# Own-side attention scores of the edges from three bf16 parts and a bf16 one-hot instead of fp32

## The reference

```python
h_all  = einsum('nf,rof->rno', x, W).reshape(8, n, 8, 32)    # per relation
scores = sum(h_all[type, src] * attn_src, -1) + sum(h_all[type, dst] * attn_dst, -1)
scores = where(scores > 0, scores, 0.2 * scores)
amax   = maximum(segment_max(scores, dst), 0)
w      = exp(scores - amax[dst])
out    = segment_sum(h_all[type, src] * (w / segment_sum(w, dst)[dst]), dst)
```

## Time and profile before

| what | value |
|---|---|
| median of three runs (lowest, highest) | 4628.5 us (4625.87, 4634.31) |
| the profiled execution's own time | 4635.05 us |
| its span, first to last instruction | 4633.4 us |
| mean granted TensorE clock | 0.831 |
| busy share: PE, PEld, DVE, ACT, POOL | 71%, 53%, 44%, 14%, 25% |
| relation tables, 2517 to 2725 us | PE 192.66 us busy of 208, granted clock 0.97 |
| edge attention, 2784 to 4040 us | PE 809.72, DVE 793.18, POOL 783.77 us busy of 1256, granted clock 0.70 |

### The profile page before, as it was taken

How to read it: one execution, slowest core, us unless ns; L and a number is a source line. 1 busy time by engine, 2 the same in 40 slices (tenths; PEclk the granted TensorE clock), 3 DMA queues, 4 the chain that set the end, 5 groups by cost and what they waited for, 6 DMA issues and landing times. The chain is left out here.

```text
span 4633.4 us, 52170 instructions
## 1 busy us (share of the span) xinstructions
PE 3299.1 (71%) x14322; PEld 2434.7 (53%) x14323; DVE 2036.0 (44%) x4300; ACT 655.7 (14%) x1334; POOL 1159.8 (25%) x1246
## 2 busy tenths in 40 slices
PE   0899789859939223999908981577677767737998
PEld 0666578648827222777704451455455545525555
DVE  5999700220051650000033612666666766733333
ACT  0111200020022111232201320000000000012222
POOL 2700100000010204000041407466666666200000
PEclk9999899979969656999958995677777767757999
DMA  2522244234400002112130316244444334100000
GB/s 97 225 98 95 82 142 127 85 93 130 131 10 0 0 3 104 60 56 65 50 104 36 133 79 130 82 119 119 111 116 121 115 111 118 55 32 21 14 14 28
DMA packets 311385, 383.64 MB, mean 83 GB/s; under 512 B 42672, under 2 KB 255489, under 8 KB 307841
## 3 DMA queue, kind: packets, MB, share of 16 engines
q1 hardware_dynamic: 240642, 221.16, 14.5%
q0 software_dynamic: 49040, 140.22, 10.7%
q10 hardware_dynamic: 21616, 21.21, 1.5%
HBM read 270.97 MB, written 111.53 MB: 83 GB/s over the span
## 5 line engine op out<-in xcount | busy, mean ns | idle before, releaser
L1955 POOL DMA_INDIRECT att_ring<-relation_rows,table_row x784 | 784.1, 1000 | 438.5 <-issue 223.2
L2071 PE MATMUL att_acc<-att_ring,att_onehot 128*128 128x264 f32 x1568 | 532.9, 480 | 198.1 <-issue 187.5
L2071 PEld LDWEIGHTS att_acc<-att_ring,att_onehot 128*128 128x128 f32 x1568 | 358.7, 238 | 328.9 <-issue 266.1
L446 PE MATMUL counts_acc<-onehot_lo,onehot_key 128*128 128x400 bf16 x2000 | 361.7, 336 | 43.7 <-DVE onehot_key L428 43.7
L425 DVE TENSOR_SCALAR onehot_lo<-node_ids,source_lo 128x800 bf16<-128x800 int16 x1000 | 366.0, 570 | 0.0
L446 PEld LDWEIGHTS counts_acc<-onehot_lo,onehot_key 128*128 128x128 bf16 x2000 | 267.7, 139 | 141.9 <-DVE onehot_key L428 83.4
L625 PE MATMUL agg_agg<-x_gnn,agg_slab 128*128 128x257 f32 x1250 | 278.6, 382 | 66.3 <-DMA agg_slab<-edge_counts 66.3
L625 PE MATMUL agg_agg<-xn,agg_slab 128*128 128x257 f32 x1250 | 277.8, 381 | 22.5 <-DMA agg_slab<-edge_counts 22.5
L625 PEld LDWEIGHTS agg_agg<-x_gnn,agg_slab 128*128 128x128 f32 x1250 | 238.6, 191 | 102.5 <-DMA agg_slab<-edge_counts 66.7
L2034 PE MATMUL att_po<-att_near,att_onehotT 128*128 128x64 f32 x1568 | 239.8, 308 | 66.6 <-issue 63.9
L625 PEld LDWEIGHTS agg_agg<-xn,agg_slab 128*128 128x128 f32 x1250 | 237.9, 190 | 58.5 <-DMA agg_slab<-edge_counts 22.9
(11 more groups left out here) (390 smaller groups left out, 4443.6 us busy)
## 6 DMA issues: line engine op xcount, KB each, us to landing
agg_slab<-edge_counts SPq DMA_DIRECT2D x50, 1600.0 KB, 7.4
edge_counts<-counts_out SPq DMA_DIRECT2D x100, 400.0 KB
relation_rows<-tab_out SPq DMA_DIRECT2D x25, 1056.0 KB
att_targets<-targets SPq DMA_DIRECT2D x28, 896.0 KB
wide_w<-L_ffn_W ACTq DMA_DIRECT2D x14, 1024.0 KB, 6.7
att_ring<-relation_rows,table_row POOLq DMA_INDIRECT x784
expert_rows_in<-blank_rows POOLq DMA_DIRECT2D x34, 256.0 KB
expert_rows_out<-blank_rows POOLq DMA_DIRECT2D x33, 256.0 KB
```

The lines of the kernel that those rows point to most:

```text
L446: mm = nc.tensor.matmul(acc[:, k, h, 0:HALF_LO], oh_key[:, k, :, j], oh_lo[:, k, j, h * HALF_LO:(h + 1) * HALF_LO], start=False, stop=Fals ...
L1955: nc.gpsimd.indirect_dma_start(slots(p)[:, j, :], None, rows_of, bass.IndirectOffsetOnAxis(ap=c.row[:, n:n + 1], axis=0)).then_inc(landed[ ...
L2071: mm = nc.tensor.matmul(acc[:, 0:RW], oh[:, j, :], slots(p)[:, j, :], start=j == 0, stop=False)
```

## The change

The near scores are kept as three bf16 parts whose sum is the fp32 number: the first is the score rounded to bf16, the second the rest rounded, the third what then remains. GpSimd makes them in `relation_tables` from a new buffer `rest` (three copies that cast, two subtractions, each waiting for the one before), and issues its stagings two tiles ahead of the split. The rows of `target_scores` grow from 64 fp32 to 192 bf16 numbers, and SyncE stores them after a new wait, `split`. In `attend` the one-hot `ohT` is bf16, and a chunk's product becomes three bf16 matmuls that accumulate in the same place of `po`. Nothing else of the edge attention is changed.

```diff
@@ relation_tables
-        near = g.sb(ctx, f"{name}_near", [P, 2, sc])
-        beyond = g.sb(ctx, f"{name}_beyond", [P, sc])
+        near = g.sb(ctx, f"{name}_near", [P, 2, 3, sc], BF16)
+        rest = g.sb(ctx, f"{name}_rest", [P, 2, sc])
+        beyond = g.sb(ctx, f"{name}_beyond", [P, 3 * sc], BF16)
...
             @block.gpsimd
             def _(pl):
-                def step(t, b):
+                def stage(t, b):
                     pl.wait_ge(turned, t + 1)
                     nc.gpsimd.tensor_copy(st[:, b, :], tile_of(xn, t)).then_inc(staged, 1)
-                tiles(pl, NT, step)
+
+                def parts(t, b):
+                    link = chain(pl, link_s, t * 4)
+                    pl.wait_ge(read, (t + 2) * banks)
+                    pl.wait_ge(stored[b], (t - b) * 16 + 32)
+                    link(nc.gpsimd.tensor_copy(near[:, b, 0, :], rest[:, b, :]))
+                    link(nc.gpsimd.tensor_tensor(rest[:, b, :], rest[:, b, :], near[:, b, 0, :], ALU.subtract))
+                    link(nc.gpsimd.tensor_copy(near[:, b, 1, :], rest[:, b, :]))
+                    link(nc.gpsimd.tensor_tensor(rest[:, b, :], rest[:, b, :], near[:, b, 1, :], ALU.subtract))
+                    nc.gpsimd.tensor_copy(near[:, b, 2, :], rest[:, b, :]).then_inc(split, 1)
+                stage(0, 0)
+                stage(1, 1)
+                for t in range(NT):
+                    if t + 2 < NT:
+                        stage(t + 2, t % 2)
+                    parts(t, t % 2)
...
-                    nc.scalar.copy(near[:, b, :].rearrange("p (h r) -> p r h", h=HD),
+                    nc.scalar.copy(rest[:, b, :].rearrange("p (h r) -> p r h", h=HD),
                                    po[:, nb, sc:2 * sc].rearrange("p (r h) -> p r h", h=HD)).then_inc(read, 1)
...
-                    sp.dma_start(dst_rows[ds(t * P, P), :], near[:, b, :]).then_inc(stored[b], 16)
+                    sp.wait_ge(split, t + 1)
+                    sp.dma_start(dst_rows[ds(t * P, P), :], near[:, b, :, :].rearrange("p k n -> p (k n)")
+                                 ).then_inc(stored[b], 16)
@@ attend
-        ohT = g.sb(ctx, f"{name}_onehotT", [P, PE_LEN])
-        near = g.sb(ctx, f"{name}_near", [P, 2, sc])
+        ohT = g.sb(ctx, f"{name}_onehotT", [P, PE_LEN], BF16)
+        near = g.sb(ctx, f"{name}_near", [P, 2, 3, sc], BF16)
...
-                    sp.dma_start(near[:, p % 2, :], near_rows[ds(at[p], P), :]).then_inc(near_in[p % 2], 16)
+                    sp.dma_start(near[:, p % 2, :, :], near_rows[ds(at[p], P), :].rearrange("t (k n) -> t k n", k=3)
+                                 ).then_inc(near_in[p % 2], 16)
...
                         for j in range(q * MGRP, (q + 1) * MGRP):
-                            mm = nc.tensor.matmul(po[:, j // bank, j % bank * sc:(j % bank + 1) * sc],
-                                                  ohT[:, j * P:(j + 1) * P], near[:, p % 2, :], start=True, stop=True)
+                            for k in range(3):
+                                mm = nc.tensor.matmul(po[:, j // bank, j % bank * sc:(j % bank + 1) * sc],
+                                                      ohT[:, j * P:(j + 1) * P], near[:, p % 2, k, :],
+                                                      start=k == 0, stop=k == 2)
```

More of the change, by code:

```diff
@@ L1629, in relation_tables @@
         out = g.sb(ctx, f"{name}_out", [P, 2, R, RW])
-        near = g.sb(ctx, f"{name}_near", [P, 2, sc])
-        beyond = g.sb(ctx, f"{name}_beyond", [P, sc])
+        near = g.sb(ctx, f"{name}_near", [P, 2, 3, sc], BF16)
+        rest = g.sb(ctx, f"{name}_rest", [P, 2, sc])
+        beyond = g.sb(ctx, f"{name}_beyond", [P, 3 * sc], BF16)
         pt = g.ps(ctx, f"{name}_pt", [P, 2, MMN])
         po = g.ps(ctx, f"{name}_po", [P, nb + 1, MMN])
-        staged, turned, copied, summed, read, none, none_out = (
-            g.sem(f"{name}_{s}") for s in ("staged", "turned", "copied", "summed", "read", "beyond", "beyond_out"))
+        staged, turned, copied, summed, read, link_s, split, none, none_out = (
+            g.sem(f"{name}_{s}") for s in ("staged", "turned", "copied", "summed", "read", "chain", "split", "beyond",
+                                           "beyond_out"))
         stored = [g.sem(f"{name}_stored{b}") for b in range(2)]
@@ L2431, in late_scores @@
         got = g.sb(ctx, "late_score_row", [P, RW])
-        near = g.sb(ctx, "late_score_near", [P, R * HD])
+        near = g.sb(ctx, "late_score_near", [P, 3 * R * HD], BF16)
+        whole = g.sb(ctx, "late_score_whole", [P, R * HD])
         of_type = g.sb(ctx, "late_score_type", [P, R])
@@ L2466, in _ @@
                                                 ).then_inc(linked, 1)
-                        v.wait_ge(linked, n * 4 + 1)
-                        by_head = near.rearrange("p (h r) -> p h r", h=HD)
+                        v.wait_ge(linked, n * 6 + 1)
+                        part = [near[:, k * R * HD:(k + 1) * R * HD] for k in range(3)]
+                        nc.vector.tensor_tensor(whole, part[1], part[2], ALU.add).then_inc(linked, 1)
+                        v.wait_ge(linked, n * 6 + 2)
+                        nc.vector.tensor_tensor(whole, whole, part[0], ALU.add).then_inc(linked, 1)
+                        v.wait_ge(linked, n * 6 + 3)
+                        by_head = whole.rearrange("p (h r) -> p h r", h=HD)
                         nc.vector.tensor_tensor(by_head, by_head, of_type.rearrange("p (o r) -> p o r", o=1)
                                                 .to_broadcast([P, HD, R]), ALU.mult).then_inc(linked, 1)
-                        v.wait_ge(linked, n * 4 + 2)
+                        v.wait_ge(linked, n * 6 + 4)
                         nc.vector.tensor_reduce(own, by_head, AX, ALU.add).then_inc(linked, 1)
-                        v.wait_ge(linked, n * 4 + 3)
+                        v.wait_ge(linked, n * 6 + 5)
                         nc.vector.tensor_tensor(own, own, got[:, D:RW], ALU.add).then_inc(linked, 1)
-                        v.wait_ge(linked, n * 4 + 4)
+                        v.wait_ge(linked, n * 6 + 6)
                         nc.vector.scalar_tensor_tensor(
@@ L2615, in build_program @@
     targets = nc.dram_tensor("targets", (NC * P + 2,), I16, kind="Internal").ap()
-    dst_rows = nc.dram_tensor("target_scores", (NP + P, R * HD), F32, kind="Internal").ap()
+    dst_rows = nc.dram_tensor("target_scores", (NP + P, 3 * R * HD), BF16, kind="Internal").ap()
     sums = nc.dram_tensor("target_rows", (NP + P, RW), F32, kind="Internal").ap()
```

## The result

The changed kernel takes 4699.64 us (median of 4 runs, 4694.73 to 4701.27), the kernel before 4630.86 us (4625.87 to 4634.31): ratio 1.0148, interval 1.013 to 1.0165. The forecast was 4704. The total fits; two of its three terms do not, and it is luck that their errors cancel.

A forecast was written before the change was run, and what follows sets the result against it. Taken as bound: the attention's 41.2 us periods, GpSimd's gathers (36.0 us) plus 5.2 us of pauses from held-up TensorE. Attention +70, first part +3 and tables +1.5 give +75 us on 4628.5: 4704 us, range 4585 to 4765.

The forecast's parts named there:

- Hold beside running gathers: Edge attention: while GpSimd's gathers run, TensorE's signals and issue are held up, until GpSimd stands still some 3.6 us.
- The run of 96 outgrows what TensorE can have open: Own scores of groups 3 to 6 become 96 instructions; 28 instructions, including group 5's 8 records, remain at the release.
- The size of 64: TensorE issues 64 instructions at speed behind the flip back, then one in 0.78 us.
- +2.8 us a period: Edge attention: the loop closes 2.8 us later in each counted period; this forecast had chance 0.45.
- GpSimd's second pause grows by 3.7 us ... +70 us: Attention: group 5 frees its slots at 3437.7, lengthening the pause; +2.8 us over 25 counted periods gives +70 us.
- 44 were named as the sign: Attention: flips of scores on TensorE 44 us apart would show the forecast, against 41.2 us before.
- One-hot in bf16: Attention, VectorE: the one-hot takes 0.82 us instead of 1.15, a gain of 0.33 us twice a part.
- bf16 pair: Own scores on TensorE: a load and matmul take 55 ns, 165 ns a product, gaining 1.8 us a part.
- First part: Attention's start: 168 instructions instead of 112 before the first own sum add 3 us.
- Tables: Relation tables: GpSimd's five operations a tile take 1.5 us; only the last split lies bare, +1.5 us.
- 24 of the 25 splits lie under TensorE's products: Relation tables: stagings issued two tiles ahead hide all splits but the last; uncovered they would cost 36 us.
- longer by no more than 3 us: Sign for the relation tables: that stage should grow by at most 3 us.

The follow-up runs named there:

- gather_pause: The kernel before with four GpSimd memsets, some 4 us, ahead of the gather of chunk 12 of each part: 4651.74 us, ratio 1.0068.
- plain_rows: The kernel before with blocks of 128 consecutive rows loaded by SyncE's queue instead of GpSimd's indirect gathers, output not the network's: 4360.57 us in one run.
- fp32_twice: The kernel before with each fp32 own-score product issued twice: 4807.61 us, ratio 1.0398.
- one_product_2: The changed kernel with only the first of three bf16 products per chunk, in the third series: 4610.82 us, ratio 1.0003 to the kernel before.
- after_spread: The changed kernel with own-score groups 1 to 4 ahead of the flip back, only 5 and 6 behind: 4718.66 us, ratio 1.0203 to the kernel before.
- tables_only: The changed table stage with the edge attention of the kernel before, fp32 scores stored as well: 4465.69 against 4427.02 us, ratio 1.0084.
- after_cut: The changed kernel with VectorE's four wide table operations cut into 25 pieces each: 4402.2 us, ratio 0.9946 to the kernel before, first series.

## Why the prediction was right in its sum and wrong in its terms

- **Hold beside running gathers: right**, by gather_pause and plain_rows. That it is there in some series only was in no trace of before.
- **The run of 96 outgrows what TensorE can have open: right** in kind (fp32_twice, one_product_2). The size of 64 from the flip back on was not: only 50, 4 of the flip and 46 of the run, are issued at speed in the changed kernel. Instructions ahead of the flip back are probably still open; after_spread shows that they count. Counted from the last TensorE product that VectorE had seen, the number issued at speed is 64 in the earlier trace rows, 64 in fp32_twice, 68 in after_spread and 90 in the changed kernel, in the periods shown. What goes beyond 64 may have been done before the hold began, so a store of 64 is neither confirmed nor ruled out.
- **+2.8 us a period: the step "GpSimd's second pause grows by 3.7 us ... +70 us" failed in size.** Measured +31.6 us in all, 1.2 a period, with flips 42.4 us apart where 44 were named as the sign. In 11 of 25 middle periods the pause is what was forecast. But behind the release the 16 records of groups 5 and 6 took 4.95 us, not 6.6 at the low clock, and `flip` came 6.3 us behind VectorE's start of L2166 at 3440.41 where 10 were forecast and 5.9 stood before. In the other periods an earlier pause, mostly at chunk 8, ends a first hold, and the second mostly costs 4.8 to 5.8 us.
- **One-hot in bf16:** 0.69 us instead of 1.15 (forecast 0.82). Its worth, if any, lay elsewhere: GpSimd's gathers took 13.2 us less over the 784, most likely because they collide with it less.
- **bf16 pair:** 12 in 0.51 us, 43 ns, forecast 55; the work saved is hidden.
- **First part:** +1.4 us, forecast 3.
- **Tables: the step "24 of the 25 splits lie under TensorE's products" failed**, 32.9 us instead of 1.5. Five operations of 64 columns do take 1.6 us (forecast 1.5), but not beside VectorE's wide operations, which I had not looked at, since they are in no line of the diff. tables_only gave +38.7 us, and cutting the wide operations gave back 37 of the 241 us. The sign "longer by no more than 3 us" had failed.

The attention's term was 38 us too high and the tables' 31 too low. They cancelled by luck. A rival "tables" of +33 us belonged into the range and was missing.

**Open:** what holds TensorE's signals and instructions back, why one series is free of it, and how many instructions may be open. Not tried: plain transfers on GpSimd's queue or gathers of consecutive rows, which would tell what in the gathers does it, VectorE's pieces with a wait for its semaphore behind every few, and the split on another engine.

## What to carry to other kernels

Before giving GpSimd a chain of small operations, look in the same stretch for VectorE operations over thousands of columns with both inputs in SBUF, and at the greatest duration of GpSimd's present ones, not the median: each link of the chain can cost one whole VectorE operation. Splitting a product into three cheap ones triples what TensorE has to issue; where its signals come late, that number and not its busy time sets what waits. And compare only kernels that ran side by side: the same kernel differed by 204 us between two series, and the attention's part of the change was about -22 us in one (an estimate) and +36 in another.

## What the runs showed of the hardware

- Beside indirect gathers from GpSimd, TensorE's signals came up to 15 us late in the periods of the kernel before (52 us in its first part), and TensorE issued one instruction in 0.7 to 0.8 us; it ended 3.3 to 3.8 us after the gathers stopped. In another series the same program ran 204 us faster without that.
- GpSimd, shut out by VectorE, was not let in between VectorE instructions of 0.6 us that follow at once (9.5 us of waiting over some 16 of them in after_cut), but at VectorE's next wait for its semaphore; from then on the two took turns.
